# A graph network on one core: some destination tiles of three aggregations summed from gathered rows instead of a dense count matrix

## The reference, cut to what matters

```
def _sage_conv(x, src, dst, Wl, bl, Wr, n_nodes):
    msgs = x[src]
    agg = jax.ops.segment_sum(msgs, dst, num_segments=n_nodes)
    deg = jax.ops.segment_sum(jnp.ones(src.shape[0], x.dtype), dst, num_segments=n_nodes)
    mean = agg / jnp.maximum(deg, 1.0)[:, None]
    return mean @ Wl.T + bl + x @ Wr.T
...
# second convolution
out = _sage_conv(h, src, dst, conv2_Wl, conv2_bl, conv2_Wr, n)
...
# three hops (self loops appended)
norm = dinv[src] * dinv[dst]
h = x
for _ in range(K):          # K = 3
    h = jax.ops.segment_sum(norm[:, None] * h[src], dst, num_segments=n)
return h @ W + b
```

## Time and profile before

| what | us |
|---|---|
| median of 3 runs (9289.38 to 9297.74) | 9289.8 |
| the profiled execution: its time | 9297.53 |
| the profiled execution: its span | 9295.6 |
| second convolution, first to last product of the counts | 1178.3 to 1794.3 |
| second hop, the same | 8098.4 to 8642.1 |
| third hop, the same | 8646.7 to 9276.8 |

### The profile page before, as it was taken

The page is one execution under the profiler, slowest core; times in us unless marked ns, Lnnn a source line. Parts: engine busy times, 40 slices in busy tenths (PEclk is TensorE's granted clock), DMA queues, the critical chain, the costliest instruction groups (busy, mean ns, idle before and its releaser), DMA issues.

```text
span 9295.6 us, 165844 instructions
## 1 busy us (share of the span) xinstructions
PE 5847.5 (63%) x64897; PEld 5071.9 (55%) x64897; DVE 2786.7 (30%) x4913; ACT 1277.2 (14%) x1585; POOL 3571.9 (38%) x3542
## 2 busy tenths in 40 slices
PE   6999899834444444435775345555455545699999
PEld 6999699722222222224765234444444444699998
DVE  6999411100000000003873233333233333311111
ACT  4777400000000000001443000000000000000000
POOL 2111000066666666665531655555555555200000
PEclk9999899866666666667995566666666666899999
DMA  4444188722222222223321122222222222499887
GB/s 128 183 182 183 63 257 256 210 64 68 68 68 68 68 68 66 67 67 82 113 83 28 23 72 71 75 75 75 74 72 74 72 68 75 141 291 290 261 256 227
DMA packets 522673, 1099.41 MB, mean 118 GB/s; under 512 B 150990, under 2 KB 330192, under 8 KB 509440
## 3 DMA queue, kind: packets, MB, share of 16 engines
q1 hardware_dynamic: 216192, 767.24, 26.0%
q10 hardware_dynamic: 197184, 211.90, 7.2%
q0 software_dynamic: 108896, 114.33, 6.2%
HBM read 871.53 MB, written 221.62 MB: 118 GB/s over the span
## 4 chain that ended last, share of the span: by engine, by line
PE 37%; another core or an unknown queue 21%; issue 19%; DVE 4%; POOL 3%; ACT 1%; DMA 1%; DVEq 1%; ACTq 0%; POOLq 0%; SPq 0%; PEldq 0%
PE banks L832 18%; PE banks L928 9%; PE banks L938 5%; POOL gath L333 3%; PE banks L351 2%; PE banks L507 1%; DVE oneh L989 1%; DVE area L1699 1%; DVE area L1727 1%; DMA gath<-tab_l,idx 1%; PE banks L519 1%; ACT gath L1306 1%; PE banks L499 1%; DMA gath<-counts 0%
## 5 line engine op out<-in xcount | busy, mean ns | idle before, releaser
L333 POOL DMA_INDIRECT gath<-tab_l,idx x3328 | 3145.4, 945 | 3443.3 <-DMA idx<-src_idx 1197.0
L1458 PE MATMUL banks<-area,ones 128*128 128x448 f32 (+1 forms) x1040 | 686.8, 834 | 1446.9 <-DVE area L1699 1269.5
L1458 PEld LDWEIGHTS banks<-area,ones 128*128 128x128 f32 x1040 | 310.5, 314 | 1791.4 <-issue 1790.6
L928 PE MATMUL banks<-area 128*128 128x128 f16 x4802 | 577.3, 248 | 890.7 <-issue 889.6
L928 PEld LDWEIGHTS banks<-area 128*128 128x128 fp8e4 x4802 | 358.8, 108 | 1094.0 <-issue 1090.1
L938 PE MATMUL banks<-oneh,gath 128*64 128x128 f32 x3328 | 598.0, 358 | 430.2 <-DMA gath<-tab_l,idx 325.8
L1699 DVE TENSOR_TENSOR area<-gath,banks 128x448 f32<-128x448 f32 (+1 forms) x256 | 138.8, 583 | 2350.3 <-remote 2281.0
L938 PEld LDWEIGHTS banks<-oneh,gath 128*64 128x64 f32 x3328 | 556.1, 191 | 461.1 <-DMA gath<-tab_l,idx 330.8
L792 ACT CAST wide<-banks 128x784 uint16<-128x784 f32 x784 | 650.4, 857 | 223.6 <-PE banks L749 223.6
L761 PE MATMUL banks<-feat,wide 128*128 128x129 f16 x9604 | 671.3, 220 | 0.3 <-ACT wide L792 0.3
L832 PE MATMUL banks<-wide,gath 128*128 128x128 f16 x9604 | 580.0, 224 | 45.2 <-issue 25.1
(11 more groups left out here) (234 smaller groups left out, 6159.2 us busy)
## 6 DMA issues: line engine op xcount, KB each, us to landing
gath<-counts SPq DMA_DIRECT2D x294, 784.0 KB, 4.4
oneh<-counts SPq DMA_DIRECT2D x294, 784.0 KB, 4.5
counts<-wide SPq DMA_DIRECT2D x98, 1568.0 KB, 5.2
gath<-counts ACTq DMA_DIRECT2D x98, 784.0 KB
area<-counts ACTq DMA_DIRECT2D x98, 784.0 KB
area<-edge_feat SPq DMA_DIRECT2D x128, 448.0 KB
gath<-tab_l,idx POOLq DMA_INDIRECT x3328
edge_h<-area ACTq DMA_DIRECT2D x128, 416.0 KB
```

The source lines that it names most:

```text
L333: pool.indirect_dma_start(out=to[:, h, c, 0:H], out_offset=None, in_=table[:, :], in_offset=bass.IndirectOffsetOnAxis(ap=idx[:, slot, c:c ...
L928: last = T.matmul(to, part_in[u].bitcast(f8)[:, t, s * P:(s + 1) * P], block_rows[:, k % 2, s, :, :].rearrange("p a f -> p (a f)"), start= ...
L1458: ins = T.matmul(bank[n][:, 0:(hi - lo) * H], ones[:, :], src[:, lo:hi, :].rearrange("p c f -> p (c f)"), start=first and lo == 0, stop=la ...
```

## The change

In each pass of two blocks three of the 14 tiles, numbers 4, 9 and 13 (in the last three passes of the second hop only 4 and 13), are no longer multiplied with their counts. Their edges are a run of the sorted edge list, at most 19 chunks of 128 (`RUN`). For such a tile:

- GpSimd gathers for each of the 19 chunks the 128 source rows (both float16 parts, 256 bytes a row) from a table in DRAM, `near_rows[k]`, one indirect DMA a chunk;
- DVE writes a one-hot matrix of 128 x 2432 in float16 (`is_equal` of the edge's destination with the node number), and multiplies it by the unit of the counts;
- PE does 19 matmuls of 128x128 by 128 columns, one-hot times gathered rows, into the bank.

There are three slots for such tiles. The tables are written by ACT's DMA queue: for the second convolution in one transfer of 12,544 rows once `rows2` is complete, for the hops one block at a time as the blocks' parts are finished. The edge lists of the 21 tiles are loaded once, at the start of the second convolution (SP, 42 small DMAs), and a further check on the device, that every tile's run fits in 19 chunks, is joined to the check that exists. The picked tiles' counts tiles are still built, but not loaded any more. The second hop's loops are written out over 14 tiles instead of two.

```
+PICKS, CHUNKS = (4, 9, 13), 19
+RUN = CHUNKS * P
+PICKED = [2 * TB * i + t for i in range(DITERS) for t in PICKS]
...
+KINDS = [kinds_of((0, DITERS, (0, 1, 2))), kinds_of((0, 4, (0, 1, 2)), (4, DITERS, (0, 2))),
+         kinds_of((0, DITERS, (0, 1, 2)))]
...
+        def picked_product(pe, k, kind, i, r, to, end):
+            hold(pe, p_near[k].onehot, 2 * kind.picked(i, r) + 2)
+            hold(pe, p_near[k].rows_in[r], 16 * CHUNKS * (i + 1))
+            for c in range(CHUNKS):
+                last = T.matmul(to, pick_oh[k][r][:, c, :], pick_rows[k][r][:, c, :], start=(c == 0 and end),
+                                stop=(c == CHUNKS - 1))
+            last.then_inc(p_near[k].summed, 1)
...
+        def slot_free(eng, k, kind, i, r):
+            hold(eng, p_near[k].summed, kind.picked(i, r) + 4 - len(kind.picks))
+        def picked_in(pool, k):
+            pool.wait_ge(g_tab, TABLED[k])
+            for kind in KINDS[k]:
+                for i in range(kind.lo, kind.hi):
+                    for r in kind.picks:
+                        slot_free(pool, k, kind, i, r)
+                        for c in range(CHUNKS):
+                            pool.indirect_dma_start(
+                                out=pick_rows[k][r][:, c, :], out_offset=None, in_=near_rows[k][:, :],
+                                in_offset=bass.IndirectOffsetOnAxis(ap=pick_src[:, 3 * i + r, c:c + 1], axis=0))\
+                                .then_inc(p_near[k].rows_in[r], 16)
+        def picked_onehot(dve, k, kind, i, r):
+            shape = [P, CHUNKS, P]
+            slot_free(dve, k, kind, i, r)
+            V.tensor_tensor(pick_oh[k][r], iota_h.rearrange("p (o w) -> p o w", o=1).to_broadcast(shape),
+                            pick_dst[:, bass.ds(3 * i + r, 1), :].rearrange("p m (c o) -> p (m c) o", o=1).to_broadcast(shape),
+                            ALU.is_equal).then_inc(p_near[k].onehot, 1)
+            hold(dve, p_near[k].onehot, 2 * kind.picked(i, r) + 1)
+            V.tensor_scalar(pick_oh[k][r], pick_oh[k][r], COUNT_UNIT, None, ALU.mult).then_inc(p_near[k].onehot, 1)
+        def onehots_beside(dve, k):
+            kind = KINDS[k][0]
+            return [(2, lambda i: [picked_onehot(dve, k, kind, i, r) for r in (0, 1)]),
+                    (65, lambda i: picked_onehot(dve, k, kind, i, 2))]
         def times_counts(pe, k, src):
-            with pe.Fori(0, TITERS) as i:
-                for u in range(2):
...
+            for kind in KINDS[k]:
+                with pe.Fori(kind.lo, kind.hi) as i:
+                    for t in range(2 * TB):
+                        hold(pe, h_red[k - 1], 2 * TB * i + t + 1)
...
+                        either_product(pe, k, kind, i, t, to, parts[src], False)
...
+            for kind in KINDS[k]:                      # hop_dve
+                with dve.Fori(kind.lo, kind.hi) as i:
+                    for t in range(2 * TB):
+                        for r in kind.picks:
+                            if t == (0, 1, 5)[r]:
+                                picked_onehot(dve, k, kind, i, r)
+                        tile(kind, i, t)
...
+        def block_out(act, k, b, of):
+            act.dma_start(near_rows[k][bass.ds(b * BN, BN), :].rearrange("(t p) c -> p t c", p=P),
+                          of[:, bass.ds(b * TB, TB), :, :].rearrange("p t a f -> p t (a f)")).then_inc(g_tab, 16)
...
+                for m, j in enumerate(PICKED):         # SP, ahead of counts_in(0)
+                    at = sp.value_load(run_at[:, j:j + 1], min_val=0, max_val=P * FC - RUN)
+                    for to, flat in ((pick_src, src_flat), (pick_raw, dst_flat)):
+                        sp.dma_start(to[:, m, :], flat.rearrange("p c -> (p c)")[bass.ds(at, RUN)]
+                                     .rearrange("(p c) -> p c", c=CHUNKS)).then_inc(g_list, 16)
...
+                act.wait_ge(y_top, 9)
+                act.dma_start(near_rows[0].rearrange("(t p) c -> p t c", p=P), rows2.rearrange("p t a f -> p t (a f)"))\
+                    .then_inc(g_tab, 16)
...
+                with act.Fori(0, DITERS) as i:         # ACT, during the second hop
+                    for h in range(2):
+                        hold(act, h_dve[0], 4 * TB * (2 * i + h + 1))
+                        block_out(act, 2, 2 * i + h, parts[0])
```

More of the change, by code:

```diff
@@ L448, in halves, with turns @@
             return [t[lo:hi, h, j * HB:(j + 1) * HB] for j in range(2)]
-        def turns(eng, d, steps, place=lambda step: step, period=None):
+        def turns(eng, d, steps, place=lambda step: step, period=None, beside=()):
             period = period or d.steps
@@ L801, in counts_in, with tile @@
         def counts_in(sp, k, each=None):
-            def tile(i, u):
+            def tile(kind, i, o):
+                u, g = kind.buffer[o], kind.ordinal(i, o)
+                back = 2
+                if kind.buffer[0] == kind.buffer[-1] and o < 2 and not isinstance(i, int):
+                    back = 1 if o == 0 else 3
                 for half in range(2):
                     words = slice(half * TW // 2, (half + 1) * TW // 2)
-                    hold(sp, h_mm[k], 2 * (2 * i + u) + half + 1)
+                    hold(sp, h_mm[k], 2 * (g - back) + half + 5)
@@ L815, in block_of @@
-            def block_of(i, h):
-                for t in range(TB):
-                    half, u = divmod(TB * h + t, 2)
-                    tile(TB * i + half, u)
-            for h in range(2):
-                block_of(0, h)
-            with sp.Fori(1, DITERS) as i:
-                for h in range(2):
-                    block_of(i, h)
-                    each(i, h)
-        def product(pe, k, i, u, to, of, end):
-            for half in range(2):
-                hold(pe, h_in[u][half], 16 * (k * TITERS + i + 1))
-                for t in range(half * NT // 2, (half + 1) * NT // 2):
-                    last = T.matmul(to, tile_in[u].bitcast(f8)[:, t * P:(t + 1) * P],
-                                    of[:, t, :, :].rearrange("p a f -> p (a f)"),
-                                    start=(t == 0 and end), stop=(t == NT - 1))
-                last.then_inc(h_mm[k], 1)
-            return last
@@ L838, in times_counts, with pair @@
-        def times_counts(pe, k, src):
-            with pe.Fori(0, TITERS) as i:
-                for u in range(2):
-                    hold(pe, h_red[k - 1], 2 * i + u + 1)
-                    to = bank[u][:, 0:2 * H]
-                    T.matmul(to, ident_h[:, 1, :], parts[src][:, bass.ds(2 * i + u, 1), :, :]
-                             .rearrange("p t a f -> p (t a f)"), start=True, stop=False)
-                    product(pe, k, i, u, to, parts[src], False)
-            if k < 2:
-                pe.wait_ge(h_mm[k], 4 * TITERS + 4)
-                pe.sem_inc(h_mm[k + 1], 4)
+            def pair(kind, i):
+                n = len(kind.dense)
+                order = [1, 0, *range(2, n)] if kind.buffer[0] == kind.buffer[-1] and not isinstance(i, int) else range(n)
+                for h in range(2):
+                    for o in order:
+                        if kind.dense[o] // TB == h:
+                            tile(kind, i, o)
+                    if each is not None and not isinstance(i, int):
+                        each(i, h)
@@ new lines, in counts_in, with product @@
+            for kind in KINDS[k]:
+                if kind.lo == 0:
+                    pair(kind, 0)
+                with sp.Fori(max(1, kind.lo), kind.hi) as i:
+                    pair(kind, i)
+        def product(pe, k, kind, i, t, to, of, end):
+            o = kind.dense.index(t)
+            u = kind.buffer[o]
+            for half in range(2):
+                hold(pe, h_in[u][half], 16 * (LOADS[k][u] + kind.loads(i, o) + 1))
+                for s in range(half * NT // 2, (half + 1) * NT // 2):
+                    last = T.matmul(to, tile_in[u].bitcast(f8)[:, s * P:(s + 1) * P],
+                                    of[:, s, :, :].rearrange("p a f -> p (a f)"),
+                                    start=(s == 0 and end), stop=(s == NT - 1))
+                last.then_inc(h_mm[k], 1)
```

184 lines of the change are left out of this document (146 added, 38 removed).

## The result

The changed kernel takes **10334.1 us** (median of 4 runs, 10328.9 to 10346.0) against 9289.6 (4 runs): ratio **1.1124** [1.1108, 1.1141], slower by 11 per cent. The prediction was 9170, faster by 1.3. The profiled execution has a span of 10344.1 us.

The account below looks back on a forecast made before the run. PE was taken to bound all three stages, with POOL coming within a tenth. Stage terms -49 - 12 - 76, checks +4, clock and DMA +12 gave -121, from 9297.5 to 9176; median-adjusted prediction 9170 us, range 9105 to 9260.

Parts of the forecast that it names:

- PE's way: PE's own time per stage with picked tiles shortened: 523 us in the convolution, 537 third hop, 64.3 a second-hop pass.
- Picked tile 1.06 us: On PE, a picked tile's 19 matmuls of 56 ns take 1.06 us, against 5.47 for a dense tile.
- PE saves: PE saves 4.4 us a picked tile: 93, 79 and 93 us in the three stages, 265 if this were all.
- POOL's pace of 1.25: On POOL, gathers follow each other at 1.25 us, so a picked tile's 19 need 23.7 us.
- `is_equal` of 2.7 us: On DVE, writing a picked tile's one-hot of 2432 columns takes 2.7 us, taken over an alternative of 1.4.
- POOL held by DVE: Two-operand DVE operations delay gathers: 1.9 + 0.3 us a picked tile; the multiplication by the unit was taken to add nothing.
- first rival: The multiplication by the unit blocks POOL too, 1.3 us a tile; POOL bounds all three stages: 9240 us, chance 0.16.
- fourth rival: The multiplication takes as long as the `is_equal` and blocks POOL wholly; the stages about cancel: 9300 us, chance 0.06.
- Start of POOL in the convolution: Second convolution: POOL's gathers wait for the table's DMA and begin 6 to 30 us after PE's start, taken as 20.
- PE's wait for the first tile: Second convolution: PE waits 23.6 us for the first picked tile's rows.
- Second rival: DVE does not get in POOL's way, POOL at 23.7 us a tile, PE bounds: 9121 us, chance 0.16.
- Third rival: Gathers slow down where DMA is 0.8 to 0.9 busy; at 1.45 us each 9380 us; chance 0.09.

Follow-up runs that it names:

- B: Kind of chip, not a run: the kernel before takes 9290 to 9360 us there, and PE crawls while POOL gathers.
- experiment 2: Kernel before plus 399, 342 and 399 unused GpSimd gathers in the three stages: ratio 1.0003 on A; 10922.7 against 9361.5 us, 1.167, on B.
- experiment 1: Changed kernel without its 1140 gathers, picked tiles' rows zeroed once per stage, on A: 7828.0 against the kernel before's 8068.4 us, 0.970.
- A: Kind of chip, not a run: the kernel before takes 8066 to 8077 us there, and no crawl is seen.
- g2's repeat: Second run of the kernel before with unused gathers at a lower rate (171, 228, 171 in the three stages), on A: 8074.4 against 8077.1 us.
- experiment 4: Kernel before, second hop's loop 14 tiles long, 171 gathers or plain transfers: 1.0031 to 1.0035. Edit in second hop only, short body, on B: 1.042.

## Why the prediction was wrong

The step that failed is "PE's way": 616 - 93 = 523 us in the convolution, 537 in the third hop, 11 x 5.55 + 3 x 1.1 a pass in the second hop. It takes a dense tile's 5.5 us from stages without a gather into stages with them; what the gathers cost PE was put at nothing, without a row. On B the gathers at 1.25 us hold PE at one product in up to 2.80 us, and 1140 of them, unused, cost 1561 us, 1.37 each (experiment 2). Each of the 60 gathered tiles brings 24 us of gathers, in which PE does next to nothing; 57 gathers a pass take 71 us, and a pass took 980 / 7 = 140, those plus nearly its own 77 again. The wait for an engine I looked for on both sides of POOL; that POOL's gathers could slow PE where PE waits for nothing of POOL's, I never asked. The Trainium skill, "SBUF — State Buffer", section "Who interferes with whom", has as its single rule that only the port pair of DVE and GpSimd causes contention; nothing in it would have warned me, and experiment 2 goes against it as a rule for what may run beside a gather.

The other terms, by their own measure:
- Picked tile 1.06 us: 1.22 with the overlap of 0.16, held.
- PE saves 3 per cent of the kernel without gathers (experiment 1): 240 us, against 265 from which the checks' 4, the second hop's branches and waits go. Stages of 531, 487 and 517 us stand beside a PE's way of 523, about 504 and 537; on A the step that failed on B held.
- POOL's pace of 1.25 held, and the `is_equal` of 2.7 us is 2.69.
- POOL held by DVE, by the `is_equal` and not by the multiplication (first rival). Timeline of DVE and POOL:

```profile
1666.22 2.69 DVE L951 TENSOR_TENSOR wide<-kept 128x2432 f16<-128x2432 f16 x1
1666.39 3.59 POOL L943 DMA_INDIRECT wide<-near_rows,kept  x1 [0.30 <-issue]
1669.06 0.80 DVE L955 TENSOR_SCALAR wide<-wide 128x2432 f16<-128x2432 f16 x1
```

The gather ends at 1669.98, 1.07 us after L951's end and only 0.12 after L955's. Had L955 held it for its length, it would have ended some 0.8 later. So the value taken, nothing, was right within 0.25 us, and the multiplication takes 0.80 us, not the 1.3 and 2.7 of the first and the fourth rival. Over all gathers of the edit on A the mean is 1065 ns beside a median of 947, 2.2 us more for a tile's 19; the forecast had 1.9 + 0.3.
- Start of POOL in the convolution: 33.1 us after PE's (1214.4 against 1181.3), taken as 20 within 6 to 30; PE's wait for the first tile 33.4, taken as 23.6.
- Second rival, PE bounds alone: on A PE waits for gathered rows 54.5 us in the convolution, in nine waits. It fell.
- Third rival, gathers slower where DMA is busy (its 44 us later in the second hop are 38 by its own terms, and the 11 of the first rival are 8; nothing rests on them): on A, at a DMA share of 0.89, POOL's pace is the same (358 gathers and 341.24 us in the window of experiment 2, 0.953 each). It fell.
- Sum: on A the three stages took 581, 538, 555 us, 36, 6 and 77 less than the 617, 544 and 632 of g2's repeat, the kernel before with gathers that cost nothing; forecast 49, 12 and 76 less. The ratio 0.986 there stands beside the forecast's 0.987. The forecast described a chip of the other kind. That is no excuse: the trace of before was of kind B and showed it.

What is open is the mechanism. Shown on B: indirect gathers, whatever they move, hold up PE when they come 1.60 us apart or closer, and the more the closer they come; PE can go on for 4 to 10 us after the first gather (for 128 products in experiment 4) before it stands, and needs 3 us to recover; the products that do issue take 0.27 us each, and start about 0.7, 1.4, 2.1 or 2.8 us apart (2.80 in the steady crawl); DVE keeps its pace. So it is the start of PE's instructions that is held up and not their execution. That each gather takes, for some 1.5 us, something that PE needs for each of its instructions, and that PE lives on a store of them at first, is an inference from this and is not shown. The instruction loads which the profile names are not it, since loops without them crawl as well. Nor is it shown what sets the two kinds of chip apart.

## What to carry to other kernels

Before giving GpSimd gathers to do beside TensorE, look in the same trace for a stretch where both already run, and compare a product's pace there with one where GpSimd rests; "issue" before single matmuls is the sign. Time the gathers alone, added and unused, before writing what uses them. If a chip shows the crawl, keep indirect gathers 2 us apart (1.6 still cost the second hop a fifth of its pace), or use plain transfers; and don't judge such an edit on one chip, for here it is 1.4 per cent faster on one kind and 11 slower on the other.

## What the runs showed of the hardware

- Chips differ: the kernel before takes 8066 to 8077 us on three of them and 9290 to 9360 on the others, and the 1225 us between them lie in the stages with gathers.
- Unused gathers at 1.25 us each: TensorE issues one product in 2.80 us on B, and at full pace on A. VectorE's small operations keep their pace on B. Plain transfers from the same queue, every 0.5 us, do nothing to TensorE.
- A DVE operation with two SBUF operands delays the gather that starts beside it on both kinds (3.59 us on B, 3.55 on A, in place of 0.94).
- A loop body of 14 tiles instead of two costs the second hop 38 us on A and 39 on B, for six branches back.
- A loop of six products with addresses from a register: 0.2 us a product, 0.34 us a turn, 25.6 us for a tile that takes 5.6 written out; the granted clock there stood at 0.50, the 1.2 GHz level.
